# Trace multipliers laid out on all partitions by loads, the products moved to ScalarE and GpSimd

## The reference

```
ctx    = causal_ema(x, tau_ctx)
gated  = x * sigmoid([x, ctx] @ Wg + bg)
h1     = gelu(x @ Wn1 + bn1)
mod    = 0.5 + sigmoid(h1 @ Wn2 + bn2)            # one value per token for each of 16 traces
traces = causal_ema(gated * mod[..., d], tau[d])  # for d in 0..15
temporal = sum_d traces[d] * softmax(blend)[d]
soma   = gelu(x @ Wsoma + bsoma)
x = x + layernorm((soma * sigmoid(temporal @ Wtemp + btemp)) @ Wout)
x = x + pooled attention (one score per token)
x = x + mixture of 8 experts and a shared one     # 3 matmuls each, hidden size 1024
x = x + head (hidden size 1024)
```

## Time and profile before

| | |
|---|---|
| median of 3 runs | 2884.26 us (2881.23 to 2886.41) |
| profiled execution | 2885.2 us, of which span 2883.4 us |
| PE busy | 2823.0 us (98%), 13018 matmuls |
| DVE busy | 1844.7 us (64%) |
| ACT busy | 1393.8 us (48%) |
| POOL busy | 1235.9 us (43%) |
| DMA | 201.22 MB |

### The profile page before, as it was taken

One profiled execution on the slowest core, in us unless ns is written; L12 is line 12 of the kernel. 1 busy time (PEld: TensorE's weight loads), 2 busy tenths in 40 slices (PEclk: granted clock), 3 DMA queues, 4 the chain that ended last, 5 costly groups with the idle time before them and its releaser, 6 DMA issues.

```text
span 2883.4 us, 36551 instructions
## 1 busy us (share of the span) xinstructions
PE 2823.0 (98%) x13018; PEld 2334.1 (81%) x13018; DVE 1844.7 (64%) x3017; ACT 1393.8 (48%) x2410; POOL 1235.9 (43%) x950
## 2 busy tenths in 40 slices
PE   8699999999999999999999999999999999999998
PEld 5488888788888888888888888888888888888887
DVE  8699778867777766556766666655766563333443
ACT  4544555455336633454534553354643463333554
POOL 5256434643454445433554245542455333333333
PEclk9799999999999999999999999999999999999999
DMA  4143322333112311111211221111221121111231
GB/s 150 50 122 97 92 92 79 112 92 95 58 48 74 116 45 45 48 56 46 91 48 48 61 83 44 48 55 47 84 67 52 48 88 57 44 44 44 70 112 39
DMA packets 85557, 201.22 MB, mean 70 GB/s; under 512 B 10296, under 2 KB 27136, under 8 KB 85376
## 3 DMA queue, kind: packets, MB, share of 16 engines
q1 hardware_dynamic: 82240, 190.38, 21.6%
q0 software_dynamic: 2560, 8.39, 0.9%
q10 hardware_dynamic: 576, 0.11, 0.0%
HBM read 190.75 MB, written 8.09 MB: 69 GB/s over the span
## 4 chain that ended last, share of the span: by engine, by line
PE 88%; DVE 7%; issue 2%; ACT 2%; POOL 1%; DMA 1%; SPq 0%; DVEq 0%; ACTq 0%; POOLq 0%
PE bank L546 19%; PE bank L548 19%; PE bank L547 19%; PE ps_out L546 9%; PE ps_out L548 9%; PE ps_out L547 9%; DVE w_lo L1134 2%; PE bank L539 1%; DVE trace L1064 1%; DVE trace L1056 1%; PE bank L620 1%; DVE hid L1158 0%; PE ps_out L539 0%; DMA stat<-mod_rows 0%; ACT L856 0%
## 5 line engine op out<-in xcount | busy, mean ns | idle before, releaser
L1297 POOL TENSOR_TENSOR hid_lo<-hid,hid_hi 128x512 fp32r<-128x512 f32 x640 | 864.9, 1352 | 1581.4 <-ACT hid_hi L943 1581.0
L546 PE MATMUL bank<-res_lo,w_hi 128*128 128x512 f32 x2432 | 962.3, 396 | 7.6 <-issue 3.5
L548 PE MATMUL bank<-res_hi,w_hi 128*128 128x512 f32 x2432 | 952.5, 392 | 0.0
L547 PE MATMUL bank<-res_hi,w_lo 128*128 128x512 f32 x2432 | 951.5, 391 | 0.0
L1158 DVE TENSOR_TENSOR hid<-hid,bank 128x512 f32<-128x512 f32 x576 | 394.0, 684 | 539.5 <-PE bank L548 510.5
L915 ACT ACTIVATE hid<-bank 128x512 f32<-128x512 f32 x576 | 344.3, 598 | 662.7 <-PE bank L548 662.2
L1134 DVE TENSOR_TENSOR w_lo<-w_raw,w_hi 128x768 fp32r<-128x768 f32 (+2 forms) x520 | 511.5, 985 | 182.5 <-ACT w_hi L884 141.7
L884 ACT ACTIVATE w_hi<-w_raw 128x768 fp32r<-128x768 f32 x392 | 331.5, 846 | 526.9 <-PE ps_out L548 505.7
L548 PEld LDWEIGHTS bank<-res_hi,w_hi 128*128 128x128 f32 x2432 | 458.1, 188 | 103.0
L546 PEld LDWEIGHTS bank<-res_lo,w_hi 128*128 128x128 f32 x2432 | 458.3, 188 | 101.1 <-issue 8.9
L547 PEld LDWEIGHTS bank<-res_hi,w_lo 128*128 128x128 f32 x2432 | 458.7, 189 | 86.4
(11 more groups left out here) (179 smaller groups left out, 1634.8 us busy)
## 6 DMA issues: line engine op xcount, KB each, us to landing
w_raw<-in_chunks SPq DMA_DIRECT2D x392, 384.0 KB, 3.0
w_raw<-in_head_chunks SPq DMA_DIRECT2D x64, 224.0 KB, 2.5
x_in<-in_xT SPq DMA_DIRECT2D x16, 256.0 KB, 3.7
out_yT<-acc SPq DMA_DIRECT2D x8, 512.0 KB, 2.8
pre_x<-in_xT SPq DMA_DIRECT2D x14, 256.0 KB, 7.0
soma_rows<-pre_soma SPq DMA_DIRECT2D x14, 256.0 KB, 2.0
soma<-soma_rows SPq DMA_DIRECT2D x14, 256.0 KB, 3.2
acc<-in_sidew SPq DMA_DIRECT2D x2, 512.0 KB, 7.0
```

Source lines behind the costliest of these rows:

```text
L546: mm(out, wh, xl, start=start and i == 0, stop=False, skip_group_check=not lone)
L547: mm(out, wl, xh, start=False, stop=False, skip_group_check=not lone)
L548: last = mm(out, wh, xh, start=False, stop=end, skip_group_check=not lone)
L1297: nc.gpsimd.tensor_tensor(hid_lo[i % DEPTH][:], hid[i % 3][:], f(hid_hi[i % DEPTH][:]), ALU.subtract).then_inc(s_hlo, 1)
```

## The change

Blocks 1 to 7 no longer use L620's matmul, `mod_pair` or piece 5's three DVE instructions. The modulation's affine step is made by POOL in block 0 before the rows go to DRAM (`pre`, 14 small instructions). In a block, SP loads two rows `d` at a time onto all 128 partitions (`spread`, 8 loads for each lane and block, 112 in all, 2 KB a partition), into the four tiles `one_hi`, `one_lo`, `two_hi`, `two_lo`, which are free between the gate's matmuls and piece 25. ACT writes gated times blend weight (`weigh`, two instructions per trace), POOL multiplies by the row (`mul`), DVE only scans, POOL adds as before. The trace buffers become a ring of four. The price of a trace piece is 2.5 for blocks 1 to 7, that of piece 5 is 0. Block 0 stays as it was.

```diff
     if 7 <= j < 7 + ND:
-        return 2.1
+        return 2.5 if b else 2.1
...
+    "act": [f"weigh{d}" for d in range(ND)],
+    "pool": ["mul0", "mul1", "mul2"] + [x for d in range(2, ND + 1) for x in [f"add{d - 1}"] + [f"mul{d + 1}"] * (d + 1 < ND)],
...
+        mod_on = [[t[s][:].bitcast(fp32) for t in (one_hi, one_lo, two_hi, two_lo)] for s in range(BB)]
+        ring = [trace[s] + [ema[s]] for s in range(BB)]
...
                 elif k == 3:
-                    sp.wait_ge(pre_act, 3 * u + 3)
-                    sp.dma_start(mod_rows[u], pre_mod[u % 3][0:ND, :]).then_inc(s_store[u % 3], 16)
+                    sp.wait_ge(pre_pool, u + 1)
+                    sp.dma_start(mod_rows[u].rearrange("(d t) -> d t", d=ND), pre_mod[u % 3][0:ND, :]).then_inc(s_store[u % 3], 16)
...
-                sp.dma_start(stat[s][0:ND, :], mod_rows[u]).then_inc(s_back[s], 16)
+
+            def spread(b, s, i):
+
+                u = (b - 1) * BB + s
+                sp.dma_start(mod_on[s][i % 4].rearrange("p h t -> p (h t)"),
+                             mod_rows[u, 2 * i * S:2 * (i + 1) * S].partition_broadcast(P)).then_inc(s_on[s][i % 4], 16)
+
+            def modulation(b, s, j):
+                if j == 6:
+                    sp.wait_ge(l_pe[s], pe_at(s, b, "gate"))
+                    for i in range(4):
+                        spread(b, s, i)
+                elif j in (8, 10, 12, 14):
+                    sp.wait_ge(l_pool[s], pool_at(s, b, f"mul{j - 7}"))
+                    spread(b, s, j // 2)
...
-                if ahead and j in (2, 3, 4):
+                if ahead and (j in (2, 3, 4) or 7 <= j < 7 + ND):
                     return
...
+            def weigh(b, s, d):
+                if d >= ND:
+                    return
+                if d == 0:
+                    act.wait_ge(l_dve[s], dve_at(s, b, "gated"))
+                elif d == 4:
+                    act.wait_ge(l_dve[s], dve_at(s, b, "scan0"))
+                elif d > 4:
+                    act.wait_ge(l_pool[s], pool_at(s, b, f"add{d - 4}"))
+                for h in range(DH):
+                    last = activate(ring[s][d % 4][:, h, :], gated[s][:, h, :], ACT.Copy, scale=bl[:, h, d:d + 1])
+                last.then_inc(l_act[s], 1)
...
+                elif 6 <= j < 7 + ND and b:
+                    for d in (0, 1) if j == 6 else (j - 5,):
+                        weigh(b, s, d)
...
                 elif 7 <= j < 7 + ND:
                     d = j - 7
-                    tr = trace[s][d % 3]
+                    tr = ring[s][d % 4] if b else trace[s][d % 3]
+                    if b:
+                        if d == 0:
+                            dve.wait_ge(l_act[s], act_at(s, b, "alpha"))
+                        dve.wait_ge(l_pool[s], pool_at(s, b, f"mul{d}"))
+                        for h in range(DH):
+                            last = V.tensor_tensor_scan((temporal[s] if d == 0 else tr)[:, h, :],
+                                                        ps[:, S + d:S + d + 1].broadcast_to([P, S]),
+                                                        tr[:, h, :], 0.0, ALU.mult, ALU.add)
+                        last.then_inc(l_dve[s], 1)
+                        return
...
+                if b and 6 <= j < 6 + ND:
+                    d = j - 6
+                    i = d // 2
+                    pool.wait_ge(l_act[s], act_at(s, b, f"weigh{d}"))
+                    if d % 2 == 0:
+                        pool.wait_ge(s_on[s][i % 4], 16 * (2 * (b - 1) + i // 4 + 1))
+                    row = mod_on[s][i % 4].rearrange("p h t -> p (h t)")[:, d % 2 * S:(d % 2 + 1) * S]
+                    nc.gpsimd.tensor_tensor(ring[s][d % 4][:], ring[s][d % 4][:], row.unsqueeze(1).broadcast_to([P, DH, S]),
+                                            ALU.mult).then_inc(l_pool[s], 1)
+
+            def pre(u, k):
+                if k == 3:
+                    pool.wait_ge(pre_act, 3 * u + 3)
+                    TS(pre_mod[u % 3][0:ND, :], pre_mod[u % 3][0:ND, :], 0.5, 1.0, ALU.mult, ALU.add).then_inc(pre_pool, 1)
```

More of the change, by code:

```diff
@@ L250 @@
 SIDE_POOL = [f"add{d}" for d in range(1, ND)]
+FROM_DRAM = {
+    "act": [f"weigh{d}" for d in range(ND)],
+    "pool": ["mul0", "mul1", "mul2"] + [x for d in range(2, ND + 1) for x in [f"add{d - 1}"] + [f"mul{d + 1}"] * (d + 1 < ND)],
+}
 SPLITS = {"x_hi", "ctx_hi", "t_hi", "p_hi", "q_hi", "x_lo", "ctx_lo", "t_lo", "p_lo", "q_lo", "xT_lo", "probT_lo"}
 def stages_in(stages, s, b):
-    if 1 <= b <= PRE and stages is not SIDE_DVE:
-        return [x for x in stages if x not in ("h1", "soma", "mod")]
+    if 1 <= b <= PRE:
+        if stages is SIDE_POOL:
+            return FROM_DRAM["pool"]
+        gone = ("h1", "soma", "mod", "mod_hi", "modpair")
+        left = [x for x in stages if x not in gone and not x.startswith("mix" if stages is SIDE_PE else "mul")]
+        if stages is SIDE_ACT:
+            k = left.index("alpha") + 1
+            left[k:k] = FROM_DRAM["act"]
+        return left
     if b:
@@ L410, in residual_stack_kernel @@
         s_back = [sem(f"pre_back{s}") for s in range(BB)]
+        s_on = [[sem(f"mod_in{s}_{i}") for i in range(4)] for s in range(BB)]
         s_y = [sem(f"y_out{i}") for i in range(NACC)]
@@ L518, in _ @@
                     pre_back(x[1], x[2])
+                elif x[0] == "side" and 6 <= x[3] < 7 + ND and 1 <= x[1] <= PRE:
+                    modulation(*x[1:])
                 elif x[0] == "side" and x[3] == 0 and x[1] + 1 < NBLK:
@@ L1032, in side @@
                 elif j == 5:
[L1033 to L1036, removed]
+                    if b:
+                        return
+                    dve.wait_ge(l_act[s], act_at(s, b, "mod"))
                     TS(mod, mod, 0.5, 1.0, ALU.mult, ALU.add).then_inc(l_dve[s], 1)
@@ L1060, in side @@
                     if d == 0:
-                        dve.wait_ge(l_act[s if b else 0], act_at(s if b else 0, b, "alpha"))
-                    decay = ps[:, S + d:S + d + 1] if b else lead_alpha[:, d:d + 1]
+                        dve.wait_ge(l_act[0], act_at(0, b, "alpha"))
+                    decay = lead_alpha[:, d:d + 1]
                     for h in range(DH):
@@ L1291, in side @@
                         pool.wait_ge(l_pool[s], pool_at(s, b, f"add{d - 1}"))
[L1292 removed]
+                    nc.gpsimd.tensor_tensor(temporal[s][:], temporal[s][:], (ring[s][d % 4] if b else trace[s][d % 3])[:],
                                             ALU.add).then_inc(l_pool[s], 1)
+                if b and 6 <= j < 6 + ND:
[11 more added lines that the diff above has]
+                    TS(pre_mod[u % 3][0:ND, :], pre_mod[u % 3][0:ND, :], 0.5, 1.0, ALU.mult, ALU.add).then_inc(pre_pool, 1)
             def late(i):
```

15 lines of the change are left out of this document (10 added, 5 removed).

## The result

The changed kernel takes **2929.14 us** (2927.36 to 2931.22), the kernel before in the same session 2883.74. The ratio is 1.0161, with a 95% interval of 1.0147 to 1.0174: it is **1.6% slower**, where 2868 and "faster" had been forecast. The profiled execution has a span of 2926.2 us against 2883.4.

A forecast was written before the change was run, and what follows sets the result against it. PE, 98% busy, was taken as the bound: matmuls by their spacing plus about 20 us idle. 2885.2 - 26.9 - 4 + 10 + 4 = 2868.3, taken as 2868 us after adjusting to the median; range 2846 to 2900.

The forecast's parts named there:

- its likeliest range: Whole kernel: the forecast case's own span, 2856 to 2878 us around 2868, chance 0.42.
- The load: Piece 6: POOL's first product waits for late rows, 0.3 us for each of 14, 4 us (0 to 20).
- its own refutation: Forecast wrong if PE waits mostly on DVE's `hid`, or POOL's wait for loaded rows exceeds 8 us a lane.
- slack 7.4 us: Expert steps: `hid_lo` may be 7.4 us late before PE wants it; 3.1 us in a head.
- The products: POOL's 224 products at 1.394 us, sharing an exclusive SBUF path with DVE: PE loses about 10 us (0 to 20).
- three heads: Heads of blocks 0, 2 and 4: POOL and DVE work exceeds PE's by 8, about 6 and about 6 us.
- The matmuls: PE, blocks 1 to 7: 224 passes of L620 at 0.12 us go, 26.9 us less.
- the waits at L620: PE's 4.9 us of waits for scans at the selector's matmul go too, counted as 4 us.
- ACT's copies: ACT: 448 scaled copies at 0.40 us, 179 us on an engine with 1490 idle; cost 0, up to 3 us.
- A: Slower: DVE's `w_lo` starves behind POOL's backlog and PE waits; 2900 us with 8 more episodes; chance 0.23.
- B: No change, 2885 us: loads and heads cost their upper ends, 20 + 10 or 10 + 20, against 31; chance 0.17.
- C: Faster, 2848 us: DVE's 212 us of room also recovers PE's other idle time, heads cost nothing; chance 0.18.

The follow-up runs named there:

- the fastest version: The changed kernel with trace rows loaded before the lane needs them, trace pieces at 2.5 and piece 5 at 1.0: 2855.55 us, ratio 0.9914.
- experiment 8: The changed kernel with early loads, ACT's copies cut to 2 of 256 columns each: 2883.89 us, against 2884.69 with whole copies.

## Why the prediction was wrong

Step by step the runs lead from the kernel before to the changed one, each with its term in the sum:

| | measured, us | the prediction's term |
|---|---|---|
| kernel before | 2882.3 | 2885.2 |
| matmuls gone, copies and transfers there, products cut, loads early, old prices | 2844.8 (-37.5) | -26.9 - 4 |
| the products | 2870.5 (+25.7) | +10 |
| the loads late | 2898.0 (+27.5) | +4 |
| the new prices | 2929.1 (+31.2) | none |

The steps depend on the order in which they are taken, as the experiments show; none of the last three was below 14 us in any order that was run.

**The step that failed first** is one that the sum doesn't have: the prices. I read the new order only to see where products, sums and low parts fall, and gave no term to what two numbers move for work that the change doesn't touch. Piece 5's instructions were gone, so I took its zero price for bookkeeping. But a price is also a distance: it keeps what follows apart. At trace pieces of 2.5 it cost 23.5 us in the kernel before (2882.4 to 2905.9) and 54.4 in the changed one (2874.7 to 2929.1); the distance from piece 36 to 38 is 22 of these 54, the rest is open. With it left at 1.0 the time is 2874.7, with the forecast's sign and inside its likeliest range of 2856 to 2878. That would have been luck: the dearer trace piece, which the sum doesn't have either, gives 23 us there (2898.0 to 2874.7), and covers most of what the load and the products cost beyond their terms. With both prices as before, the changed kernel takes 2898.0, slower than the kernel before: the next two terms would have made the forecast wrong without any new price.

**The load** had a term, 4 us with 20 as its bound. It measured 44 us in the kernel as it stands, 27 at the old prices and 19 at 2.5 and 1.0, always with the products in place. The wait itself was sized nearly right, 4 to 8 us a lane against 9.3, past the 8 that the prediction named as its own refutation. What failed is who waits behind it: I followed POOL's queue (`hid_lo`, slack 7.4 us) and not DVE's, where the first scan holds up the other lane's end and with it PE's attention matmul.

**The products** had 10 us (0 to 20) and measured 26 early, at the old and at the new prices, and 52 late. Their mean of 1.53 us was within the bounds; `w_lo` rose only from 1.143 to 1.199. So the exclusion of POOL and DVE is real, but I charged it only to three heads, and only where the sum of the work passed PE's. It also lengthens DVE's small chains, L1145 from 0.88 to 1.06 us in the mean and L1149 from 0.49 to 0.56, more where a lane starts, as above, and those chains had one step to end in. How much of the 26 us comes by this way and how much by `hid`, `hid_lo` and the weight loads, no run separates. That the upper bound held neither term shows how it was built: each was bounded by itself, with the rest of the kernel punctual.

**The matmuls** had 26.9 us; about 34.7 by the accounting above, and the 37.5 of the table with the waits at L620. The spacing of the 256-column pass alone isn't its price: the passes behind it are stretched. I had taken 0.227 from a stretch without L620. **ACT's copies** at 0 were right, by experiment 8.

**The rivals.** A comes nearest in time and sign (2900, slower), but its mechanism isn't what decided: four `w_lo` above 3 us where it wanted over eight, PE's largest wait (8.97 us) isn't on `hid_lo` behind such a spell, and the fastest version has spells as long. B had the load and the products as costs, at their upper ends, and even these were too low. C's 2848 is about what is left when the products are cut away at the old prices, 2844.8.

## What to carry to other kernels

A price, priority or due time that changes with an edit is an edit of its own: put it alone into the old kernel before anything else, since here one number was worth more than the whole loss. When an instruction may be late, follow the queue behind it on *every* engine that waits for it, up to the next thing that PE needs, and take the distance in steps to that. And costs of lateness don't add up: the load, the products and the new prices cost 44, 52 and 31 us when each is taken away from the whole, 127 in sum; early loads, cut products and the old prices together gave 84 (2929.1 to 2844.8).

## What the runs showed of the hardware

- A changeover from one GpSimd instruction to the next doesn't always let a waiting VectorE instruction in: two `w_lo` of 0.95 us stood 16.51 us while twelve GpSimd instructions ran without a gap.
- Small VectorE instructions on SBUF alone are held up by a busy GpSimd too: a pair of TENSOR_SCALAR of 128x256 took 2.50 us at 402.73, 0.49 each as a mean before, and a TENSOR_TENSOR of 128x2 took 5.32 us at 1707.03 while four GpSimd instructions ran, where 0.15 is its time in most places of the trace.
- PE pays for a wait twice. After the gap of 6.57 us that ended at 543.90 the granted clock is 0.50 for 4.1 us, the lower level of 1.2 GHz, and passes of 512 columns start 0.427 us apart; then it is back near 1.00 and they start 0.23 apart. Passes at this level are most of the 16 us above. Not every wait brings it: behind the 2.50 us that ended at 142.95 the granted clock stays at 1.00. The stretch (columns of the earlier trace rows):

```profile
543.90:548.00 4.10, 4.10 (x10) 3.23 (x11) 2.96 (x4) 4.08 (x8) 3.10 (x3) 0.50 0.52 132
548.00:552.00 4.00, 4.00 (x21) 3.37 (x20) 2.90 (x5) 3.63 (x7) 4.00 (x3) 0.97 0.71 239
```

- Two rows of DRAM, 2 KB together, read by 128 partitions (256 KB) land in 3.5 us as a median in `one_hi`, the first of a lane's four loads, and in 3.7 to 4.4 in the other three, against 3.2 for a plain transfer of that size.
